# Perceiver layer on one core: in the delta-rule projection, value chunks ahead of gate chunks, and the first two triangular solves in larger shares beside the gate chunks

## What is computed

```
qkv = x @ w_qkv;  z = (x @ w_z)                       # 64 + 32 blocks of 128 columns
beta = sigmoid(x @ w_b);  g = -exp(a_log) * softplus(x @ w_a + dt_bias)
q, k, v = split(silu(causal_conv4(qkv)))              # 16 q heads, 16 k heads, 32 v heads of 128
A = where(strict, -(k_beta @ k.T) * decay, 0)         # per head, 64 x 64
attn = solve_triangular(I - A, I)                     # per head
v_new = attn @ (v * beta)
o = where(lower, (q @ k.T) * decay, 0) @ v_new
out = rms_norm(o) * norm_w * silu(z);  return out @ w_out
```

## Time and profile before

| | us |
|---|---|
| median of 3 runs | 2776.75 (2775.61 to 2778.75) |
| the profiled execution, its own time | 2778.05 |
| its span, first to last instruction | 2776.3 |
| TensorE busy | 2639.8 (95%) |
| VectorE busy | 1766.5 (64%) |
| ScalarE busy | 1529.8 (55%) |
| GpSimd busy | 502.1 (18%) |
| mean granted TensorE clock | 0.984 of full speed |

### The profile page before, as it was taken

How to read it: one execution, slowest core, us unless ns; L and a number is a source line. 1 busy time by engine, 2 the same in 40 slices (tenths; PEclk the granted TensorE clock), 3 DMA queues, 4 the chain that set the end, 5 groups by cost and what they waited for, 6 DMA issues and landing times.

```text
span 2776.3 us, 38769 instructions
## 1 busy us (share of the span) xinstructions
PE 2639.8 (95%) x13810; PEld 2192.9 (79%) x13810; DVE 1766.5 (64%) x3857; ACT 1529.8 (55%) x2992; POOL 502.1 (18%) x428
## 2 busy tenths in 40 slices
PE   6879999999999999999999999999999879998999
PEld 5668788888887887887887887878777669777887
DVE  7855636546546546546455466668669866668997
ACT  7944435435435435445444355437686567856776
POOL 4402102002002012011011020015353332022111
PEclk9989999999999999999999999999999999999999
DMA  3533013022022021030030121435675642549996
GB/s 126 137 98 104 18 43 104 11 61 85 15 77 65 20 85 49 24 94 30 27 100 16 40 85 48 149 123 162 171 214 168 155 95 67 187 186 366 377 372 226
DMA packets 255054, 317.85 MB, mean 114 GB/s; under 512 B 128712, under 2 KB 166216, under 8 KB 241808
## 3 DMA queue, kind: packets, MB, share of 16 engines
q1 hardware_dynamic: 251392, 310.03, 35.3%
q0 software_dynamic: 3040, 5.08, 0.7%
q10 hardware_dynamic: 432, 0.27, 0.0%
HBM read 274.22 MB, written 46.98 MB: 116 GB/s over the span
## 4 chain that ended last, share of the span: by engine, by line
PE 80%; DVE 10%; ACT 3%; DMA 2%; issue 2%; SPq 1%; POOL 1%; POOLq 0%; DVEq 0%; ACTq 0%
PE ps L103 21%; PE ps L105 21%; PE ps L104 21%; PE ps L887 3%; PE ps L843 3%; PE ps L915 2%; DVE lnw L2171 2%; DVE zz L2174 2%; PE ps L868 2%; DVE cv L2138 1%; PE ps L908 1%; PE ps L1346 1%; PE ps L1345 1%; PE ps L2012 1%; ACT qn L380 1%
## 5 line engine op out<-in xcount | busy, mean ns | idle before, releaser
L1246 POOL TENSOR_TENSOR lnw<-lnw,half 128x8 f32<-128x8 f32 x88 | 144.4, 1641 | 1202.4 <-DVE lnw L981 1202.4
L103 PE MATMUL ps<-whf,cth 128*128 128x512 f32 (+1 forms) x832 | 335.9, 404 | 0.0
L103 PE MATMUL ps<-cnh,pth 128*128 128x512 f32 (+1 forms) x832 | 330.1, 397 | 1.4 <-issue 1.4
L105 PE MATMUL ps<-whf,ctl 128*128 128x512 f32 (+1 forms) x832 | 325.9, 392 | 0.0
L104 PE MATMUL ps<-wlf,cth 128*128 128x512 f32 (+1 forms) x832 | 325.5, 391 | 0.0
L104 PE MATMUL ps<-cnl,pth 128*128 128x512 f32 (+1 forms) x832 | 324.9, 390 | 0.0
L105 PE MATMUL ps<-cnh,ptl 128*128 128x512 f32 (+1 forms) x832 | 324.7, 390 | 0.0
L2664 DVE TENSOR_TENSOR ml<-mr,mh 128x2048 fp32r<-128x2048 f32 x90 | 203.3, 2287 | 26.6 <-ACT mh L2606 26.6
L1157 ACT ACTIVATE pr<-ps,sm 128x1601 f32<-128x1601 f32 x56 | 89.7, 1601 | 210.0 <-DVE sm L1023 210.0
L1182 ACT ACTIVATE xo<-ps 128x128 f32<-128x128 f32 x64 | 17.8, 278 | 312.7 <-PE ps L915 312.7
L1042 DVE TENSOR_TENSOR ptl<-ps,pth 128x512 fp32r<-128x512 f32 (+1 forms) x256 | 139.1, 585 | 79.0 <-ACT pth L1169 78.6
(11 more groups left out here) (352 smaller groups left out, 6398.4 us busy)
## 6 DMA issues: line engine op xcount, KB each, us to landing
mr<-in_moe SPq DMA_DIRECT2D x90, 1024.0 KB, 7.0
ctr<-in_ctxt SPq DMA_DIRECT2D x96, 256.0 KB, 2.7
pr<-in_ctxn SPq DMA_DIRECT2D x96, 256.0 KB
wv<-in_wv SPq DMA_DIRECT2D x64, 256.0 KB, 2.8
wr<-in_wqkv SPq DMA_DIRECT2D x64, 256.0 KB, 2.9
wvf<-in_wattn SPq DMA_DIRECT2D x11, 1024.0 KB, 5.1
ca<-cat_d SPq DMA_DIRECT2D x16, 512.0 KB, 3.9
qk_d<-cv SPq DMA_DIRECT2D x32, 256.0 KB, 3.2
```

What stands on the lines that cost most here:

```text
L103: pe.matmul(dst, lh, rh, start=first, stop=False)
L105: return pe.matmul(dst, ll, rh, start=False, stop=last)
L1246: po.tensor_tensor(rs[0:w, s, :], nv[0:w, s, :], half[0:w, 0:8], ALU.pow).then_inc(kx_rs, 1)
```

## The change

Value blocks take the steps 32 to 63, directly behind the keys, and gate blocks the steps 64 to 95. Solve 0 keeps its start at step 63, but its budget for a step is 1300 (600 where a "second" lies in the step) in place of 800 (170), and it must end by step 76 (before: 83). Its result is stored at step 76 (before: 84). The coefficients of solve 1 are loaded at step 79 (before: 84); the solve runs from step 81 (before: 88), and must end by step 93, where its result is stored. Before, its last part stood in the back phase, and its result was stored at t = 4. Nothing is added or dropped: each engine has the same operations. Only ScalarE's table loads, which are put in where the function changes, become two fewer, 16 for 18 in the whole program.

```diff
-        GATE_PLACES, VALUE_PLACES, place = [], [], 32
-        for k in range(32):
-            if k not in (6, 12, 18, 24):
-                GATE_PLACES.append(place)
-                place += 1
-            VALUE_PLACES.append(place)
-            place += 1
-        GATE_PLACES += list(range(place, NPOS))
+        VALUE_PLACES, GATE_PLACES = list(range(32, 64)), list(range(64, NPOS))
...
-                if 63 <= s < 83:
-                    yield from some(steps, 170 if burst < 4 and 4 <= r < 8 else 800)
-                if s == 83:
+                if 63 <= s < 76:
+                    yield from some(steps, 600 if burst < 4 and 4 <= r < 8 else 1300)
+                if s == 76:
                     yield from steps
-                if s == 84:
                     yield "solved", 0, 0
+                if s == 79:
                     yield "system", 1, 0
                     steps = solving(1)
-                if 88 <= s < NPOS:
-                    yield from some(steps, 700 if s < 92 else 2000)
+                if 81 <= s < 93:
+                    yield from some(steps, 1100)
+                if s == 93:
+                    yield from steps
+                    yield "solved", 1, 0
...
-            squares, fetched, solved_to = 0, 3, 0
+            squares, fetched, solved_to = 0, 3, 1
...
-                if t in (4, 14, 22):
+                if t in (14, 22):
                     yield from steps
-                    solved_to = (4, 14, 22).index(t) + 1
+                    solved_to = (14, 22).index(t) + 2
                     yield "solved", solved_to, 0
```

## The result

The changed kernel took 2781.64 us in the median of 16 runs (2778.99 to 2784.41), the kernel before 2775.46 beside it. The ratio is 1.0022 (95% interval 1.0014 to 1.0030): 6 us or 0.2% slower, little, but clear of the noise. I had predicted 2770 and gave slower 0.20.

A forecast was written before the change was run, and what follows sets the result against it. TensorE was taken as the bound nearly everywhere, VectorE's solve 0 delaying it from 2062 to 2143. Steps losing 14.4 us for 16.3 win 1.9, the back phase 5: 2778.05 becomes 2771.2, 2769.9 against the median; forecast 2770, range 2765 to 2774.

The forecast's parts named there:

- the clock's: In the projection steps, one wait long enough to halve TensorE's clock: 1.7 us lost (none to three, 0 to 5).
- Steps 32 to 63: Value steps: VectorE fits, ScalarE narrowly, 30.0 us against TensorE's 31.8 a burst; 2 us lost, bounds nothing and 6.
- rival (c): Steps 42 to 68: ScalarE's waits reach TensorE, 9 us lost, total 2777; sign: steps 32 to 63 over 119 us; chance 0.12.
- Steps 63 to 74: Solve 0 beside gates: VectorE's work outlasts TensorE's, 7.3 us lost; 3.3 without collisions.
- My upper bound of 11: Steps 63 to 74: 11 us lost if seconds take 2.19 us, the price with GpSimd beside.
- the 5.5 us of room for VectorE: Steps 64 to 73: weight slots let TensorE be two steps ahead, so 5.5 us came off the loss.
- Steps 81 to 91: Solve 1 beside gates: 1.1 us lost to VectorE's work plus a 2.3 us wait, 3.4 in all; 6.1 at worst.
- The wait for coefficients: Before solve 1, VectorE waits 2.3 us for coefficients loaded two steps ahead, every low part queued behind; 5 at worst.
- The start of the back phase: After the projection, no solve stands before the first addition of p1: 5 us won of 6.7, ends 0 and 7.
- rival (d): Back phase: loads of the solved blocks come when they did, only the 1.9 us wait goes; 2773, chance 0.10.
- rival (b): Steps 63 to 91: VectorE's pile takes over, 26 us lost for 16.3, start wins 3.5; slower, 2783, chance 0.19.
- Rival (e), the gate stores: Gate steps: three slots, a store every 2.73 us, ScalarE would hold TensorE up; given nothing of its own.

The follow-up runs named there:

- the order alone: Kernel before with values in steps 32 to 63 and gates in 64 to 95, its old solve schedule kept: 2772.39 us, 0.9988.
- smaller shares: Changed kernel with solve 0 at 800 and 170, rest at step 80, solve 1 at 900 from step 85, rest at 95: 2773.2 us, 0.9991.
- solve 1 at 800: Changed kernel with solve 1 at 800 a step up to step 94, not 1100 up to 92: 2775.78 us, 0.9999 against the kernel before.
- six gate slots: Changed kernel with six places for gate blocks instead of three, from gate block 9 on: 2783.74 us, 1.0027 against the kernel before.

## Why the prediction was wrong

The forecast was a sum: 14.4 us lost in the steps for 16.3 before, and 5 won behind them. All three of its larger terms for the steps were too small, and so was the clock's.

- **Steps 32 to 63: I took 2 us, the runs show 5.8.** This step failed, by a cause the prediction did not name: the norms in steps 35 and 36, with three banks, 4.3 us. What I did name (ScalarE in the decay steps) cost 1.5; rival (c) was wrong as long as TensorE had been held up just before, and shows only once that is repaired. Its sign, over 119 us for steps 32 to 63, did not come: they took 116.3.
- **Steps 63 to 74: 9 us with one half clock, measured 13.1.** The mechanism was right, and the four builds' collisions too (4.9 us for my 4). The sizes were not: 8.7 us of waits for my 7.3, some 2.8 of half clock for 1.7, since it lasted longer than eight matmuls, and 1.6 in gaps that no row of waits shows, to which I had given nothing. My upper bound of 11 with 1.7 just misses it. One reading is that the 5.5 us of room for VectorE that I subtracted did not carry through: its work was summed over ten steps, but the longest gaps between low parts (5.4 and 6.7 us) came in a row at the end of the burst. No run tests this apart.
- **Steps 81 to 91: 3.4 us, measured 6.3.** I had 29.8 us of VectorE work for 24.6 of TensorE and let 4.1 of lookahead pay for most. The shares of 1100 made each of steps 85 to 91 too long, 2.6 us in all; shares of 800 took 2.5 of them back. The wait for coefficients that I priced at 2.3 was 0.7, though steps 82 to 84 lost 2.0 around it. And 1.8 were step 81, by the gate stores. VectorE's 15.1 us of waits for high parts lay for the most part before solve 1 began, where TensorE waited for no low part. So the term was too small and its cause half right.
- **The start of the back phase: 5 us, measured 3.2 to 3.6.** It is 3.6 against the order alone (176.3 to 172.7), and 3.2 against before with the half clock taken off; with smaller shares it is 1.4 to 2.1, so part of it is hidden, as rival (d) had it. The addition at 7.8 us behind the last step, for 8 foretold, was right. So were the five table loads for silu and four for exp, and 10.6 us for the products of solve 1; those of solve 0 took 13.5 for 12.5.
- **The sum.** 25.3 us lost for 14.4 foretold. Between the two traces, steps 32 to 94 became 8.4 us longer (225.3 for 216.9), where I had 1.9 shorter: 10.3 too low, and 2770 + 10.3 = 2780 for 2781.6 measured. That is rival (b) in size (26 lost, 3.5 won, 2783), with a part from the norms that it did not have. I gave it 0.19.
- **Rival (e), the gate stores**: 55.5 us of waits on ScalarE, and 1.7 of them on the path, once, in step 81. Giving it nothing of its own was nearly right.
- My first half also hid a gain: the order alone was 3.9 us faster by the medians (2772.4 and 2776.3 on the same chip), 0.12% by the ratio. A small gain forecast for it alone would have been right. The loss came with the shares, which the prediction had called "near twice as large as those that made the waits".

Not settled: why the medians differ by 6.2 and the sums of the stretches, with 3.2 to 3.6 in the back phase, by 5; why solve 1 at 800 gained 6 us by the ratios and 2 in its trace; and whether the time that comes back in steps 48 and 49 is all ScalarE's.

## What to carry to other kernels

Work that is cut into portions between the steps of a pipeline must fit each step on its own: the operation that TensorE waits for, plus the portion at its price beside a busy GpSimd, has to stay under the step's time, or the ring's few places are used up in a run of steps and the clock falls too. A long wait on an engine in the chain proves nothing until it is taken away: of 55 us for stores, 1.7 held up TensorE. Whoever is busy between the two waits is the first suspect. When an order is made even, look for the one-time work (norms, tables) that the uneven order had covered.

## What the runs showed of the hardware

- After a wait of 1.85 us TensorE's matmuls ran at 0.51 of full speed for 3.3 us, after one of 3.08 us at 0.50 for at least 6.6 us. The length of the wait alone does not decide it: behind a wait of 1.96 us (before 2099.13, changed kernel) the matmuls ran at full speed, and with six gate slots the clock is 1.00 from 2082 to 2135 with a wait of 2.7 us in it. The order alone, with no wait over 1.3 us from 2082 to 2135, shows 1.00 there.
- VectorE's operations with two inputs from SBUF took 0.67 to 0.95 us for 0.4 where a GpSimd operation ran.
- Stores of the gate blocks, with three slots and one every 2.73 us, made ScalarE wait up to 8.0 us; with six slots still up to 6.9.
